# A two-layer cross-attention and mixture-of-experts kernel: the values' opening in column pieces with idle transposes, first decays among the context sums, key sums among the last units, and GpSimd in the last norm

## What is computed

```python
# layer 0 attention, per batch and head (dh = 32): q = layernorm(x), k = v = ctx
log_D = log_fg + ig                       # gates from x and ctx; "decays"
D = exp(log_D - max_log_D)
C = (q @ k.T) / sqrt(dh) * D
h = (C / (normalizer + EPS)) @ v
hn = (h - mean(h)) * rsqrt(var(h) + EPS) * ln_scale
x = x + hn
# layer 1, from the same ctx, so it can be computed early:
v_img = ctx @ vi_w + vi_b                 # (16*128, 512) @ (512, 2048)
k_img = rms_norm(ctx @ ki_w + ki_b) * nki_s
```

## Time and profile before

| | us |
|---|---|
| median of three runs | 1344.85 (1341.27 to 1345.71) |
| the profiled execution | 1339.19, its span 1337.5 |
| values and gates, from the profile's timeline | about 2 to 193 |
| heads and keys | about 193 to 448.6 |
| the rest | about 448.6 to 1337.5 |

### The profile page before, as it was taken

How to read it: one execution, slowest core, us unless ns; L and a number is a source line. 1 busy time by engine, 2 the same in 40 slices (tenths; PEclk the granted TensorE clock), 3 DMA queues, 4 the chain that set the end, 5 groups by cost and what they waited for, 6 DMA issues and landing times. The chain is left out here.

```text
span 1337.5 us, 24404 instructions
## 1 busy us (share of the span) xinstructions
PE 1280.8 (96%) x7358; PEld 1059.6 (79%) x7359; DVE 845.0 (63%) x1613; ACT 741.4 (55%) x1831; POOL 379.8 (28%) x353
## 2 busy tenths in 40 slices
PE   7999998999999899899999989999989999999998
PEld 6787776777777678688876778878888888988886
DVE  3545547779778963544445477553587777777965
ACT  5235448788886431454455454545785565565551
POOL 0111015273736026499131342154010000000041
PEclk9999999999999899899999999999999999999999
DMA  7896499787764484666459776564375555555403
GB/s 253 308 366 244 149 310 351 260 292 243 269 218 164 127 318 172 219 205 196 133 186 318 230 264 192 159 203 182 134 221 167 164 153 164 162 161 157 119 27 126
DMA packets 166599, 277.06 MB, mean 207 GB/s; under 512 B 29744, under 2 KB 58160, under 8 KB 166256
## 3 DMA queue, kind: packets, MB, share of 16 engines
q1 hardware_dynamic: 140704, 220.50, 51.1%
q0 software_dynamic: 8672, 29.37, 6.6%
q10 hardware_dynamic: 17136, 26.09, 5.2%
HBM read 167.11 MB, written 108.80 MB: 206 GB/s over the span
## 5 line engine op out<-in xcount | busy, mean ns | idle before, releaser
L3003 ACT ACTIVATE prob<-banks,attend_row,rq 128x128 f32<-128x128 f32 x248 | 110.5, 470 | 0.0
L3016 ACT ACTIVATE attend_ol<-banks,of_attend_vbias 128x512 fp32r<-128x512 f32 x64 | 44.2, 691 | 116.8 <-PE banks L3215 116.8
L121 PE MATMUL banks<-of_shared_split,key_lead 128*128 128x512 f32 x256 | 104.8, 409 | 4.0 <-DVE key_trail L1422 3.8
L121 PE MATMUL banks<-wo,attend_ol 128*128 (+1 forms) x256 | 106.2, 415 | 0.0
L121 PE MATMUL banks<-queries_rows_split,queries_wl 128*128 128x512 f32 x256 | 100.8, 394 | 0.0
L123 PE MATMUL banks<-wo,attend_ot 128*128 (+1 forms) x256 | 100.7, 393 | 0.0
L123 PE MATMUL banks<-of_shared_split,key_trail 128*128 128x512 f32 x256 | 100.6, 393 | 0.0
L122 PE MATMUL banks<-of_shared_split,key_lead 128*128 128x512 f32 x256 | 100.2, 391 | 0.0
L122 PE MATMUL banks<-wo,attend_ol 128*128 (+1 forms) x256 | 99.9, 390 | 0.0
L123 PE MATMUL banks<-queries_rows_split,queries_wt 128*128 128x512 f32 x256 | 99.8, 390 | 0.0
L122 PE MATMUL banks<-queries_rows_split,queries_wl 128*128 128x512 f32 x256 | 99.8, 390 | 0.0
(11 more groups left out here) (399 smaller groups left out, 3522.0 us busy)
## 6 DMA issues: line engine op xcount, KB each, us to landing
mlstm_gmax<-running_max SPq DMA_DIRECT2D x32, 512.0 KB, 6.1
k_heads<-heads_key ACTq DMA_DIRECT2D x64, 256.0 KB, 4.6
q_heads<-queries_head SPq DMA_DIRECT2D x64, 256.0 KB, 2.7
q_ahead<-q_heads SPq DMA_DIRECT2D x64, 256.0 KB, 4.2
of_attend_k<-k_heads SPq DMA_DIRECT2D x60, 256.0 KB, 4.0
of_attend_v<-v_heads SPq DMA_DIRECT2D x60, 256.0 KB, 3.2
key_raw<-in_L_xattn_ki_w SPq DMA_DIRECT2D x20, 512.0 KB, 4.8
sorted_rows<-of_shared_split SPq DMA_DIRECT2D x2, 5120.0 KB, 27.5
```

What stands on the lines that cost most here:

```text
L121: nc.tensor.matmul(out, lead_l, lead_r, start=first, stop=False)
L3003: ins = nc.scalar.activation(prob[:, j % 2, b, :], ps[:, j % 2, b * S:(b + 1) * S], ACT.Exp, bias=row[:, j % 2, 1, b:b + 1], scale=rq[:, b ...
L3016: nc.scalar.activation(ol[:, par, j, :], ps[:, 4 + j % 2, :], ACT.Identity, bias=vbias[:, bass.ds(quad_of(it) * 4 + j, 1)]).then_inc(ol_do ...
```

## The change

Four places are changed; what is computed is the same.

1. Opening of the values. The setup's instructions move into GpSimd's stream of the values' phase, and TensorE waits for the identity only. The first four batches come in four DMAs of 128 columns (512 B rows), each ahead of its weight chunk. TensorE first makes 10 transposes of the identity into bank 0 (`keep_busy`). Its order is then: turns 0, 1; chunk 0, turn 2; chunk 1, turn 3; chunk 2, turns 4 to 7; chunk 3.
2. Quad 1's weight trails are made at units 11 to 14.
3. Heads' opening. VectorE's order was four context sums, decays 0 and 1, and so on in the loop. It is now sums 0 and 1, decay 0, sums 2 and 3 (with the scaling), decays 1, 2, 3.
4. End of the heads. TensorE makes the sums of the first 12 batches in threes behind the last four key units, and those of the last four batches ahead of the third tail unit, for which it now waits for the last `add_square` before that unit. ScalarE keeps the third tail unit after the late roots. GpSimd multiplies the last group's heads by ln_scale (4 instructions, into `cmat`) once they are centred, between the second and third part of the weight split, and adds batches 2 and 3 of the last group to x. VectorE scales from `cmat` in the order 3, 2, 1, 0, makes no product by ln_scale, adds batches 0 and 1, and waits for GpSimd before the statistics of 2 and 3.

```diff
+def keep_busy(nc, bank, ident, n):
+    for _ in range(n):
+        nc.tensor.transpose(bank[:, 0:P], ident[:], ident[:])
...
-        TRAILS = {OPENS[q + 1] - (6 if q < QUADS - 2 else 5) + c: (q + 1, c) for q in range(QUADS - 1) for c in range(C)}
+        TRAILS = {OPENS[q + 1] - (6 if 0 < q < QUADS - 2 else 5) + c: (q + 1, c) for q in range(QUADS - 1) for c in range(C)}
...
-            load_ctx(0)
             for c in range(C):
+                sp.dma_start(stage[0][:, :, c * P:(c + 1) * P],
+                             a["ctx_2048"][0:GB, :, c * P:(c + 1) * P].rearrange("b s d -> s b d")).then_inc(ctx_first[c], 16)
                 sp.dma_start(raw[:, c, :], w_dram[c * P:(c + 1) * P, 0:N]).then_inc(first_loaded[c], 16)
...
-            for t in range(C):
-                turn(t)
+            pe.wait_ge(made, 1)
+            keep_busy(nc, ps[:, 0, :], K.ident, 10)
+            turn(0)
+            turn(1)
             for c in range(C):
                 first_chunk(c)
-                if c < C - 1:
-                    turn(C + c)
+                if c + 2 < C:
+                    turn(c + 2)
                 if c == C - 2:
-                    turn(C + c + 1)
+                    for t in range(C, 2 * C):
+                        turn(t)
...
+                if k == 2:
+                    pool.wait_ge(centred, G)
+                    pool.wait_ge(pv, G * QUADS)
+                    for b in range(GB):
+                        ins = nc.gpsimd.tensor_tensor(cmat[:, b].rearrange("p b s -> p (b s)"),
+                                                      piece(raw_heads(G - 1), b).rearrange("p h e -> p (h e)"), lnb[:], ALU.mult)
+                    ins.then_inc(weighed, 1)
...
             pool.wait_ge(cut_trail, len(parts))
+            pool.wait_ge(late_scaled, 1)
+            for b in range(2, GB):
+                xb = K.x[:, (G - 1) * GB + b, :]
+                nc.gpsimd.tensor_tensor(xb, xb, piece(sq, b).rearrange("p h e -> p (h e)"), ALU.add).then_inc(late_added, 1)
...
-            for b in range(GB):
-                context_sum(0, b)
+            context_sum(0, 0)
+            context_sum(0, 1)
             decayed(0, 0, True)
+            context_sum(0, 2)
+            context_sum(0, 3)
+            for n in range(1, 4):
+                decayed(0, n, True)
...
-            for b in range(GB):
+            dve.wait_ge(weighed, 1)
+            for b in reversed(range(GB)):
                 r = slice(b * H0, (b + 1) * H0)
-                ins = nc.vector.tensor_tensor(sq[:, r, :], raw_heads(last)[:, r, :],
+                ins = nc.vector.tensor_tensor(sq[:, r, :], cmat[:, b].rearrange("p b s -> p (b s)").rearrange("p (h e) -> p h e", h=H0),
                                               small[:, 5, r].unsqueeze(2).broadcast_to([P, H0, DH0]), ALU.mult)
+                if b == 2:
+                    ins.then_inc(late_scaled, 1)
             own(ins)
             finish(PER)
             out = sq[:].rearrange("p (b h) e -> p b (h e)", b=GB)
-            own(nc.vector.tensor_tensor(out, out, lnb[:].unsqueeze(1).broadcast_to([P, GB, D]), ALU.mult))
-            xg = K.x[:, last * GB:, :]
-            own(nc.vector.tensor_tensor(xg, xg, out, ALU.add))
+            xg = K.x[:, last * GB:last * GB + 2, :]
+            own(nc.vector.tensor_tensor(xg, xg, out[:, 0:2], ALU.add))
             for b in range(last * GB, B):
+                if b - last * GB >= 2:
+                    dve.wait_ge(late_added, b - last * GB - 1)
                 row_stats.batch(b)
...
+            pe.wait_ge(total_done, CLOSES[G - 2] + 1)
+            pe.wait_ge(c_done, UNITS)
             for m in range(PER - LAG, PER):
                 keys(G - 1, m)
+                token_sums(range(3 * (m - PER + LAG), 3 * (m - PER + LAG) + 3))
...
+                if b == TAIL_IN_HEADS - 1:
+                    pe.wait_ge(total_done, UNITS)
+                    token_sums(range((G - 1) * GB, B)).then_inc(sums, 1)
                 tail_unit(nc, ps, split, tail_w, b).then_inc(tail_product, 1)
-            pe.wait_ge(total_done, UNITS)
...
```

More of the change, by code:

```diff
@@ L155, in root, with setup @@
                                   ).then_inc(self.rooted, 1)
-def setup(nc, K):
-    with Phase(nc, "setup") as ph:
-        blank, made = ph.sem("blank"), ph.sem("made")
-        block = ph.block()
-        @block.gpsimd
-        def _(pool):
-            nc.gpsimd.memset(K.ident[:], 0.0).then_inc(blank, 1)
-            nc.gpsimd.memset(K.eps5[:], 1e-5)
-            nc.gpsimd.memset(K.eps6[:], 1e-6)
-            nc.gpsimd.memset(K.ones[:], 1.0).then_inc(blank, 1)
-            pool.wait_ge(blank, 2)
-            nc.gpsimd.affine_select(out=K.ident[:], in_=K.ident[:], compare_op=ALU.not_equal, fill=1.0,
-                                    base=0, pattern=[[-1, P]], channel_multiplier=1).then_inc(made, 1)
-            pool.wait_ge(made, 1)
+def setup(nc, K, pool, blank, made):
+    nc.gpsimd.memset(K.ident[:], 0.0).then_inc(blank, 1)
+    nc.gpsimd.memset(K.ones[:], 1.0)
+    nc.gpsimd.memset(K.eps5[:], 1e-5)
+    nc.gpsimd.memset(K.eps6[:], 1e-6)
+    pool.wait_ge(blank, 1)
+    nc.gpsimd.affine_select(out=K.ident[:], in_=K.ident[:], compare_op=ALU.not_equal, fill=1.0,
+                            base=0, pattern=[[-1, P]], channel_multiplier=1).then_inc(made, 1)
 class Gates:
@@ L231, in values_and_gates @@
         product, even_done, odd_done = sem("product"), sem("even_done"), sem("odd_done")
+        blank, made = sem("blank"), sem("made")
+        ctx_first = [sem(f"ctx_first{c}") for c in range(C)]
         cleared, masks = sem("cleared"), sem("masks")
@@ L357, in _ @@
             own = Own(pool, own_pool)
+            setup(nc, K, pool, blank, made)
             nc.gpsimd.memset(w_gate[:], 0.0)
@@ L588, in turn @@
                 g, c = divmod(t, C)
-                if c == 0:
+                if g == 0:
+                    pe.wait_ge(ctx_first[c], 16)
+                elif c == 0:
                     pe.wait_ge(ctx_loaded[g], 16)
@@ L817, in heads_and_keys @@
         cut_lead, cut_trail = sem("cut_lead"), sem("cut_trail")
+        weighed, late_scaled, late_added = sem("weighed"), sem("late_scaled"), sem("late_added")
         EARLY = (G - 1) * GB
@@ L1116, in keep_tail @@
                                      ).then_inc(tail_kept, 1)
-            for b in range(TAIL_IN_HEADS):
+            for b in range(TAIL_IN_HEADS - 1):
                 keep_tail(b)
@@ L1215, in body @@
                         gather(g, n // 4)
-                    if n + 1 < PER or g + 1 < G:
+                    if (n + 1 < PER or g + 1 < G) and not (first and n < 3):
                         decayed(g, n + 1, first)
@@ L1367, in _, with token_sums @@
                 body(g, False)
+            def token_sums(tokens):
+                for b in tokens:
+                    ins = nc.tensor.matmul(ps[:, 2, b:b + 1], total[:, b * S:(b + 1) * S], K.ones[:, 0:1],
+                                           start=True, stop=True)
+                return ins
+            pe.wait_ge(total_done, CLOSES[G - 2] + 1)
+            pe.wait_ge(c_done, UNITS)
             for m in range(PER - LAG, PER):
                 keys(G - 1, m)
+                token_sums(range(3 * (m - PER + LAG), 3 * (m - PER + LAG) + 3))
             pe.wait_ge(tail_loaded, 32)
@@ L1375, in _ @@
                     pe.wait_ge(ksq_done, UNITS)
+                if b == TAIL_IN_HEADS - 1:
+                    pe.wait_ge(total_done, UNITS)
+                    token_sums(range((G - 1) * GB, B)).then_inc(sums, 1)
                 tail_unit(nc, ps, split, tail_w, b).then_inc(tail_product, 1)
-            pe.wait_ge(total_done, UNITS)
-            for b in range(B):
-                ins = nc.tensor.matmul(ps[:, 2, b:b + 1], total[:, b * S:(b + 1) * S], K.ones[:, 0:1],
-                                       start=True, stop=True)
-            ins.then_inc(sums, 1)
 def mlstm(nc, K, E1, x_split, a, tail_dram, tail_w, tail_v, v_dram, split_dram, ct_dram, k_dram, rk):
@@ L3338, in two_layers @@
         K.stats, K.mv, K.rstd = kept("stats", [P, B, 6]), kept("mv", [P, B, 2]), kept("rstd", [P, B])
-        setup(nc, K)
         routed_weights = [a[f"L0_ffn_w_{n}"] for n in ("gate", "up", "down")]
```

1 line of the change is left out of this document (added).

## The result

| | before | after |
|---|---|---|
| median, us | 1344.08 (14 runs, 1341.27 to 1347.55) | 1349.69 (14 runs; 13 of them 1342.37 to 1354.69) |
| ratio | | 1.0038 (95% interval 1.0022 to 1.0053) |
| profiled execution, its span, mean clock | 1339.19, 1337.5, 0.987 | 1351.52, 1349.8, 0.983 |

One of the changed kernel's 14 runs took 1816.14 us, at a mean granted clock of 0.652, and the ratio leaves it out. The changed kernel is about 5 us slower. The forecast was no change, 1344.6, with 1349 as the range's upper end: it was wrong, and just outside its range.

What follows compares the result with a forecast made beforehand. TensorE was taken to be busy nearly all the time, so only its gaps, slow stretches and phase ends could give time back. -1.2 - 1.6 - 0.3 + 2.9 = -0.2 us gave 1344.6 us, range 1338 to 1349.

Steps and rivals of the forecast that it cites:

- (a): Opening of the values: an earlier first DMA and new order of turns start unit 4 at 23.9, gaining 1.2 us.
- (b): Quad 1's weight trails one unit later: the wait at unit 12 goes, gaining 1.6 us, bounds 0.8 to 1.6.
- chunk 0 costs 2.5 more: Bound in the opening: if the transposes don't bring the clock up, its gain turns into a loss of 1.3 us.
- everything there moves with TensorE: Said of quad 1's last weight trail: GpSimd's DMA was issued under heavy traffic, but moves with TensorE; no size given.
- have several us: In the opening: DMAs of the third and fourth group, issued at 13.9 and 19, have several us to spare.
- (c): Heads' opening, first decays among the context sums: 0.3 us gained, between a loss of 0.6 and a gain of 2.2.
- ScalarE then works without a gap to the next split of weights: Heads' opening, behind the exp released by the later mask: ScalarE has no gap and passes only some 0.3 us on.
- (d): End of the heads: work shared with GpSimd makes the next phase start 4.25 us later, 1.4 back, cost 2.9 us.
- 1.4 back: Phase behind the heads: its first tail unit runs at full clock, 2.8 us for 4.56, of which about 1.4 remain.
- The rival built on that rule: End of the heads: GpSimd's weight leads hold VectorE too, cost there 5.3 us, total 1347.1; chance 0.13.
- That the engines don't get in each other's way: Rival at the end of the heads: few collisions, 4.2 us gained there, total 1337.6; chance 0.24.
- That the clock stays down in the opening: Rival: half clock through chunks 0 and 1, unit 4 at 28.9, opening loses 3.8 us, total 1349.7; chance 0.10.

Runs made afterwards that it cites:

- e16_opening_filled_again: The same kernel as `e10_opening_filled`, run once more on another chip: ratio 0.9964 to the kernel before, median 1339.46 us.
- e2_opening_alone: The kernel before with only the change's first part, the new opening of the values: ratio 1.0046.
- e13_opening_and_trails: The kernel before with the change's first two parts, the opening and the later weight trails: ratio 0.9981.
- e10_opening_filled: Kernel before plus opening and later trails, with turns 2, 3 behind chunk 0, 4 behind chunk 1, 5 to 7 behind chunk 2, ten more idle transposes: 0.9959.
- e9_decays_gap_filled: The kernel before with only the new order of decays, plus 16 identity transposes on TensorE ahead of the fifth key unit: ratio 1.0013.
- e11_best: `e10_opening_filled` plus the new order of decays with 16 identity transposes ahead of the fifth key unit, old end of the heads: 0.9994 to the kernel before.
- e4_end_alone: The kernel before with only the change's fourth part, the new end of the heads: ratio 1.0028.
- e1_before_again: The kernel before, unchanged, measured and profiled once more: ratio 0.9997, span 1342.5 us.

## Why the prediction was wrong, step by step

The forecast was -1.2 - 1.6 - 0.3 + 2.9 = -0.2 us; the runs give about +5. By the table of parts the opening and the trails together are -2.6 (forecast -2.8), the decays +2.1 (-0.3), the end +5.5 (+2.9), each good to 2 or 3 us. The rows say 1.8 for the first two (unit 16 at 61.29, 63.13 before).

**(a) Opening: it gave nothing, where 1.2 was forecast.** That the sum of (a) and (b) came out at -2.6 is luck. "Chunk 0 at 7.4" (7.14) and the idle transposes held, and "turn 1 follows turn 0" was an unsaid step that failed: the second piece landed 1.5 us later. Lead 3 was at 15.29 instead of 13.9, and the sign named for that, unit 4 behind its old time, was met (25.12). The step that failed in size is the clock. I had it as a bound ("chunk 0 costs 2.5 more"), weighed against a forecast at full clock, and it came to 1.4 us. That by itself is the gain of 1.2: unit 4 is where it was. `e16_opening_filled_again` shows it from the other side. The step that failed in kind is "everything there moves with TensorE", for SP's load released by the fourth turn. I had priced that DMA itself ("have several us"), and not what SP has queued behind it: in `e2_opening_alone` 4.4 us late at the third group, 2.9 late at the weights, and with the old trails 4.28 us at unit 12. It isn't so each time: in the changed kernel the weights went out as before, and on the mean of six kernels the lead is 1.5 us late.

**(b) Trails: right**, 1.6 by the row. What was named as late next, the last weight trail, is late in two of the ten profiled executions with this edit (1.8 us in `e13_opening_and_trails`, 1.9 in `e10_opening_filled`), each time with the slow matmuls behind it. SP's late issue isn't the whole reason: in the second the weights went out at 32.87, as before, and VectorE waited 2.33 us for the load of x. What the DMAs lose and where is open. So my lower bound, a gain of 0.8, was too high: such an execution loses it all.

**(c) Decays: the sign was wrong.** The wait did shrink, by 2.1 us, as forecast. The fifth key unit starts no earlier for it, at 20.6 us behind the first (20.7). In the kernel before, two things held its key trail: ScalarE's lead, and VectorE, which itself stood 1.36 us for the slow outputs.

The step that failed is "ScalarE then works without a gap to the next split of weights", and with it that the mask's delay "passes only some 0.3 on" and the bound of 0.6. ScalarE does stand, for the second key unit's store: 1.18 us in the changed kernel, 1.1 to 3.1 in all six with the new order. The prediction asked what ScalarE and VectorE work on there, and not which DMA they wait for. The copy of the fourth key unit comes 1.7 us late, and with it the sixth unit, by 1.6 us (25.5 against 23.9).

The clock has a small part in it. Before, TensorE's 3.1 us gap lay ahead of 64 small matmuls, and the lower clock fell on those: scores of 2.03 and outputs of 1.82, where they are 1.17 and 1.08 in the changed kernel. These 1.6 us come back with the new order and bring nothing, for the fifth unit can't start earlier. Now the gap lies ahead of a dense unit; its slow half costs 0.4 and 0.6 us in two of six kernels and nothing in the others, and with that unit kept fast (`e9_decays_gap_filled`) the sixth was no earlier. Why kernels with the new order are another 1 us later by key unit 60 (medians of 233.2 against 230.4 from the first) is open; in `e11_best` the clock is at 0.89 in the groups behind, but nothing isolates it.

**(d) End: the mechanism was right, within 0.8 us of the rows, and its last term was mis-sized.** The centring is 1.4 us later in the execution after than in that before; with that added, the forecast had the scaling at 441.2 (440.44) and the end of the last `add_square` at 446.8 (446.63); only one of the two variance products was slowed, where two were forecast. TensorE was to be idle some 7 us (6.83), the third tail unit at 0.43, and the phase 4.25 later (4.3 against the mean of the 12). What failed is "1.4 back" for the faster start of the next phase. It is real where I looked, at the first transposes: only 2.4 us later there. But VectorE makes the normals, and it starts with the phase, 4.3 late. Before, TensorE's slow tail unit had covered for it (one wait of 0.5); now TensorE waits three times, 1.6 us, and by the first routed matmul the loss is 4.1 again. So the term is 4.1, not 2.9. The ratios say 5.5 with some 3 us of doubt; that 1.4 more are lost behind 550 us is neither shown nor excluded.

The Trainium skill (SBUF — State Buffer, "SBUF: two separate sides") has the shared ports locked for a whole instruction. For operations with two inputs the rows agree (0.22 became 1.27 beside GpSimd's trail at 436.32, 0.69 became 1.63). For GpSimd's operation with one input they don't: the `add_square` at 438.34 lies inside the weight lead of 437.59 and took 0.68, and in `e4_end_alone` one at 439.88 lies inside the lead of 439.12 and took 0.68; here the measurement decides. The rival built on that rule would have given 1347.1, nearer than my forecast, and for the wrong reason.

**The rivals.** That the engines don't get in each other's way is refuted by the row of 4.53. That the clock stays down in the opening came partly true: chunk 0 alone, not both chunks. Its price, 1349.7, is the measured median to a tenth, and that is luck: it put unit 4 at 28.9, and it stands at 25.12. None of the rivals had the store that ScalarE waits for in (c) or the normals in (d). By the ratios those two parts miss by 2.4 and 2.6 us, each good to some 3; rows show 2.0 and 1.2 of it.

## What to carry to other kernels

Removing a wait of TensorE gave nothing here, where other engines bound the stretch: the gap moved on. So look at what the next engine waits for, its DMAs too: a buffer that is stored from is free only once the store has landed, and a copy into it can wait for that with no name in the profile but "issue". If time is "given back" to the first engine of a phase, check what the second one needs, and take the difference at a place behind both. And when a turn or a copy releases a DMA, look at all that its queue has behind it, not at the DMA alone.

## What the runs showed that I had not expected

- One program differs by 5 us between two executions on the trace (spans 1337.5 and 1342.5), 3 of it behind 460 us. In the ten executions of `e1_before_again` the time goes with the mean granted clock (correlation -0.79; over the 31 executions of the kernel before that were measured beside it, -0.60).
- Ten transposes of the identity and an idle 1.52 us left the clock down for chunk 0; with eight more transposes in that gap the chunk ran 0.24 apart from its second matmul on.
- Four products by GpSimd took 3.96 at 128x496 in the heads' opening and 5.39 at 128x512 beside VectorE's chain. There VectorE lost 2.0 us in four scalings, GpSimd's two additions took 3.25 together. The sharing costs both sides.
